# One power for both norms, weight columns by head pair, a rearranged first step and a base laid under the last sum

## The chip, the cores and the metric

The kernel runs on one core of one Trainium2 chip. The metric is device time in microseconds (us) of the whole program; smaller is better. The core's engines each work through their own queue in order: TensorE (PE, with its weight loads shown apart as PEld), VectorE (DVE), ScalarE (ACT), GpSimd (POOL), and SyncE (SP), which here issues all DMAs. They meet only at semaphores.

## What is computed

One transformer layer on x of shape (8, 512, 256) in float32: attention with 16 heads of 64, then a feed-forward block of width 1024 whose output is scaled by a routing weight.

```
xn  = rms_norm(layernorm(x), gamma)          # eps 1e-5 inside the first root, floor 1e-12 on the second norm
q, k, v = split(xn @ w_qkv)                  # 256 x 3072, 16 heads of 64
x   = x + softmax(q*scale @ k.T) @ v @ w_out
y   = layernorm(x)
p   = softmax(y @ router_w); top 2 of 8, normalised; weight = their sum
x   = x + (gelu(y @ w1 + b1) @ w2 + b2) * weight
```

## The kernel before

**Number format.** Every product is made of three TensorE products: each operand is kept as a high part (rounded) and a low part (the rest), and high x high, low x high and high x low are summed in PSUM. So whatever leaves PSUM for a later product costs an ACT copy (the high part, `*_hi`) and a DVE subtraction (the low part, `*_lo`). Softmax probabilities are normalised by POOL before they are transposed.

**Stages.** Eight batches of 512 tokens go through attention one after another; x1 = x + attention is stored in DRAM; then eight batches go through the feed-forward part. Attention works in units n = 0 to 255: one pair of heads times one tile of 128 queries (scores of two heads, 512 keys each). A step holds two units. The order of each engine's queue is written out by hand: in step s, PE runs `transpose_prob(2s-3)`, `scores(2s)`, `scores(2s+1)`, `transpose_prob(2s-2)`, then a "first" auxiliary block, `weighted_values(s-2)` and the "rest" blocks. Auxiliary blocks (`plan_aux`) are the transposes of xn ("xt"), q and k of the next pair, v of the next four heads ("v"), and the product with w_out ("out"). Each has a place that names its PSUM bank (`PS_AUX`). I write t(n) for `transpose_prob(n)` and w(s) for `weighted_values`.

**Prologue.** SP loads x of batch 0 in four tiles, the columns of w_qkv of the first pairs in three groups (`first_stage`, each as two DMAs), identity and gamma, then six 128x768 pieces of w_qkv into `prob`, `wstage` and `halves_out` (which are idle until then). ACT makes high parts (L816, L821), DVE or POOL low parts (L992, L916, L936). PE runs 19 matmuls on zeros (`keep_warm`, L679), and 4 more after the transposes of xn. DVE takes statistics of four x tiles (L967, L971), writes var and var + eps (L973, L974), POOL raises them to +0.5 and -0.5 (L879), DVE makes the scale in four dependent small operations (`attention_scale`, L980 to L984), normalises four tiles (L988). PE transposes them (L574), ACT and DVE split them into `xT`, PE makes k, q, then scores. Units 0 and 1 are followed by q1, k1, both v blocks, then units 2 and 3, then t(0); t(1) waits for the second v block.

**Weights.** `slot_of_chunks` says in which half step a 128x1024 or 128x768 piece is split. Pieces 6 and 7 (w_out) are split in steps 3 and 5: high by ACT, low by POOL. `exp` of the first three units and the first two `copy_halves` wait for the pieces that lie in their buffers.

**Last stage.** For each batch c: eight `up` products, GELU on ACT, high part on POOL (L891), low part on DVE (L992); then four `down` tiles in two PSUM banks, with `transpose_x2` (L628), `route` (L639) and `transpose_logits` (L647) of the next batch between them. `finish` (L1194, L1199) adds b2 to two tiles out of PSUM, then multiplies by the routing weight and adds x1; `store_out` (L456) stores two tiles.

Of the kernel before, what the change touches and what calls it, by code (L numbers as in the profile page):

```python
# [31 lines left out]
P = 128  # L32
# [14 lines left out]
RMS_EPS = 1e-12  # L47
SCALE = DH ** -0.5
# [9 lines left out]
WARM = {FIRST_STEP: 19, -3: 4}  # L58
# [6 lines left out]
PS_AUX = {1: 4, 2: 6, 3: 7, 4: 5}  # L65
# [5 lines left out]
PS_DOWN = (5, 6)  # L71
PS_LAST_OUT = (7, 6, 5, 4)


def plan_aux():
# [3 lines left out]
    for step in range(FIRST_STEP, LAST_STEP + 1):  # L79
        b, rel = divmod(step, SPB_STEPS)  # L80
        blocks = []
        if step == -4:
            blocks += [(1, "xt", 0, 0), (2, "xt", 0, 1)]
# [31 lines left out]
def layer_kernel(nc, x, gamma_cols, w_qkv, w_out, router_w, w1, b1_cols, w2, b2_rows, ident, out):  # L115
# [10 lines left out]
    with ExitStack() as ctx:  # L126
# [20 lines left out]
        halves = sb("halves", [P, 2, TT], F32)  # L147
        ln_stats = sb("ln_stats", [P, TT, 6], F32)
        ln_mv = sb("ln_mv", [P, TT, 2], F32)
        ln_var = sb("ln_var", [P, 2, TT], F32)  # L150
        ln_pow = sb("ln_pow", [P, 2, TT], F32)
        ln_std, ln_rstd = ln_pow[:, 0, :], ln_pow[:, 1, :]
        ln_norm = sb("ln_norm", [P, 3, TT], F32)
# [39 lines left out]
        f_y = sb("f_y", [P, 2, 2, D], F32, ffn)  # L193
# [28 lines left out]
        s_gain = sem("gain_ready")  # L222
        s_q_first_hi = sem("first_query_tile_hi")
        s_q_first = sem("first_query_tile_done")
        s_wload = [sem(f"weights_loaded{i}") for i in range(6)]
# [43 lines left out]
        s_fy = sem("down_read")  # L269
# [11 lines left out]

        N_CONST = 2
        N_CHUNKS = 12

        def weight_chunk(i):

            if i < 6:
                cols, k = i // 2, i % 2
                c = slice(cols * INNER + 2 * P, (cols + 1) * INNER)
                return wqkv_v[:, k, c], [w[:, k, c] for w in wqkv]  # L290
# [9 lines left out]
        stage_of = [0, 1, 2, 3, 4, 5] + [3] * (N_CHUNKS - 6)  # L300
        nth_in_stage = [stage_of[:i].count(stage_of[i]) for i in range(N_CHUNKS)]

        POOL_CHUNKS = (0, 1, 2, 3, 4, 5, 6, 7, 8)
        POOL_HI = (8,)
        slot_of_chunks = {-6: [0, 1], -4: [2], 1: [3], 3: [4], 5: [5], 6: [6], 10: [7]}
# [16 lines left out]
        def weight_stage(i):  # L322
            stage = stage_of[i]
            if stage < NPROB:
                whole = prob[:, stage, :]
            elif stage == NPROB:
                whole = wstage[:, :]
            else:
                whole = halves_out[:, stage - NPROB - 1].rearrange("p a n -> p (a n)")
            return whole[:, 2 * P:] if i < 6 else whole  # L330

        def wait_weight_loaded(eng, i):
            eng.wait_ge(s_wload[stage_of[i]], 16 * (nth_in_stage[i] + 1))
# [7 lines left out]
        def load_weight(sp, i):  # L341
            if nth_in_stage[i]:
                wait_weight_split(sp, max(j for j in range(i) if stage_of[j] == stage_of[i]))
            sp.dma_start(weight_stage(i), weight_chunk(i)[0]).then_inc(s_wload[stage_of[i]], 16)
# [48 lines left out]
        def _(sp):  # L393
            for t in range(TT):
                sp.dma_start(xin[:, t, :], x_v[0][:, t, :]).then_inc(s_x_first[t], 16)
            for k in range(KT):
                sp.dma_start(first_stage[0][:, k], first_source[0][:, k]).then_inc(s_first_load[0], 16)
            sp.dma_start(identity[:, :], ident).then_inc(s_const, 16)
            sp.dma_start(gamma_sb[:, :], gamma_cols).then_inc(s_const, 16)
            for k in range(KT):  # L400
                sp.dma_start(first_stage[1][:, k], first_source[1][:, k]).then_inc(s_first_load[1], 16)
            for k in range(KT):
                sp.dma_start(first_stage[2][:, k], first_source[2][:, k]).then_inc(s_first_load[2], 16)
            for i in range(7):
                load_weight(sp, i)
# [18 lines left out]
            for slot in range(FIRST_SLOT, LAST_SLOT + 1):  # L424
# [25 lines left out]
                for i in weight_slots(slot - 1):  # L450
                    if 6 < i + 1 < N_CHUNKS:
                        load_weight(sp, i + 1)

            def store_out(c, part):
                sp.wait_ge(s_fo, 2 * c + part + 1)
                sp.dma_start(out_v[c][:, 2 * part:2 * part + 2], f_o[:, c % 2, 2 * part:2 * part + 2])\  # L456
                    .then_inc(s_out[c % 2], 16)
# [12 lines left out]
            for i in range(2):  # L470
                sp.wait_ge(s_out[i], 32 * (B // 2))
# [3 lines left out]
        def _(pe):  # L475
# [8 lines left out]
            def scores(n):  # L484

                pair, tile = divmod(n, TT)
                if tile == 0:
                    pe.wait_ge(s_aux, aux_index[("k", pair)] + 1)
                if n == 0:
                    pe.wait_ge(s_q_first, 1)  # L490
# [6 lines left out]
                for q_part, k_part in ((QH, KH), (QL, KH)):  # L497
                    for h in range(2):
                        rows = slice(h * DH, (h + 1) * DH)
                        pe.matmul(ps[:, PS_SCORE[n % 2] + h, :], part[rows, q_part, q0:q0 + P], part[rows, k_part, :],  # L500
                                  start=q_part == QH, stop=False)
                for h in range(2):
# [48 lines left out]

            def aux(step, block_no, place, kind, *args):
# [23 lines left out]
                elif kind in "qk":  # L576
                    pair, = args
                    base = (kind == "k") * INNER + pair % PAIRS * P
                    if pair == 0:
                        pe.wait_ge(s_first_lo, 1)  # L580
                    elif pair == 1:
                        pe.wait_ge(s_first_lo_pool, 1)
                    elif pair == 2:
                        wait_weight_split(pe, 1 if kind == "q" else 3)
                    for k in range(KT):
                        if pair == 0:
                            pe.wait_ge(s_aux, aux_index[("xt", 0, k)] + 1)
                        ins = products(bank, [w[:, k, base:base + P] for w in wqkv],
                                       [v[:, k, :] for v in xT], k == 0, k == KT - 1)
                elif kind == "v":  # L590
# [4 lines left out]
                    elif quad == 1:  # L595
                        wait_weight_split(pe, 5)
# [659 lines left out]
```

## Time and profile before

| | us |
|---|---|
| median of 3 runs | 1207.37 (1205.76 to 1207.79) |
| the profiled execution's own time | 1207.04 |
| its span in the trace | 1205.2 |
| PE busy | 1186.5 (98%) |
| DVE / ACT / POOL busy | 964.6 / 889.3 / 642.7 |

The span is that of the instructions; 1.8 us of the time lie around it. Matmuls are pipelined: a row's duration is longer than the distance to the next one, so starts, not durations, tell what a matmul costs. Attention fills the span from 12 to about 1016 us, the feed-forward part the rest.

### The profile page before, as it was taken

The page shows a single profiled execution, that of the slowest core. Times are in us where ns is not written, and L with a number is a line of the kernel's source. Part 1 is how long each engine was busy: PE and PEld are TensorE (multiplying, and loading weights), DVE is VectorE, ACT ScalarE, POOL GpSimd, SP SyncE. Part 2 cuts the span into 40 slices and gives each one's busy share as a digit, 9 for nine tenths or more (in the row PEclk, how much of TensorE's full clock was granted, in tenths as well). Part 3 has the DMA queues.
Part 4 walks back from the last instruction along what each step waited for, and adds up shares of the span by engine and source line. Part 5 has one row for each costly group of instructions (what it writes and reads, how often), then busy time and mean ns, then how long its engine had stood idle before and what let it go on. Part 6 is the DMA issues. An engine that isn't in the chain of part 4 may idle for free. (4 is left out here: it accounts for less than half of the span.)

```text
span 1205.2 us, 29229 instructions
## 1 busy us (share of the span) xinstructions
PE 1186.5 (98%) x11351; PEld 1038.2 (86%) x11351; DVE 964.6 (80%) x1745; ACT 889.3 (74%) x1921; POOL 642.7 (53%) x802
## 2 busy tenths in 40 slices
PE   8999999999999999999999999999999999999998
PEld 6778888888888888888888888888888888888987
DVE  5789888888888888888888888889888987666644
ACT  5888788878888888888888887888888883344332
POOL 4665556555655565555555655556465664222221
PEclk9999999999999999999999999999999999999999
DMA  4122111311131113111311131113111232111100
GB/s 160 36 56 69 36 36 37 88 37 36 37 88 37 36 37 88 36 36 37 88 36 36 37 88 37 36 36 89 36 36 37 71 89 75 40 59 44 36 19 35
DMA packets 33464, 62.91 MB, mean 52 GB/s; under 512 B 5808, under 2 KB 9904, under 8 KB 33328
## 3 DMA queue, kind: packets, MB, share of 16 engines
q1 hardware_dynamic: 33328, 61.05, 19.8%
q8 instruction: 91, 1.49, 0.5%
q14 instruction: 45, 0.37, 0.1%
HBM read 19.08 MB, written 8.39 MB: 23 GB/s over the span
## 5 line engine op out<-in xcount | busy, mean ns | idle before, releaser
L882 POOL TENSOR_SCALAR prob<-prob,rowinv 128x512 f32<-128x512 f32 x512 | 349.6, 697 | 297.3 <-DVE rowinv L1073 296.6
L790 ACT ACTIVATE prob<-ps,negmax 128x512 f32<-128x512 f32 x512 | 347.2, 686 | 37.8 <-DVE negmax L1068 33.8
L992 DVE TENSOR_TENSOR pT_lo<-ps,pT_hi 128x512 fp32r<-128x512 f32 (+1 forms) x384 | 320.2, 862 | 24.8 <-ACT pT_hi L781 20.2
L1068 DVE TENSOR_REDUCE negmax<-ps 128x2 f32<-128x1024 f32 x256 | 310.9, 1215 | 0.6 <-PE ps L504 0.6
L532 PEld LDWEIGHTS ps<-identity,prob 64*128 64x128 f32 x4096 | 153.8, 138 | 61.5 <-issue 17.3
L778 ACT ACTIVATE pT_hi<-ps 128x1024 fp32r<-128x1024 f32 x128 | 131.5, 1027 | 99.1 <-issue 98.6
L532 PE MATMUL ps<-identity,prob 64*128 64x64 f32 x4096 | 176.6, 226 | 6.2 <-DVE vbuf L992 4.5
L500 PE MATMUL ps<-nat 64*128 64x512 f32 x1024 | 172.4, 413 | 2.4 <-ACT prob L790 0.9
L546 PE MATMUL ps<-pT_hi,vbuf 128*128 128x256 f32 x1024 | 164.6, 283 | 2.6 <-DVE pT_lo L992 2.6
L546 PE MATMUL ps<-pT_lo,vbuf 128*128 128x256 f32 x1024 | 164.1, 283 | 0.0
L781 ACT ACTIVATE pT_hi<-ps 128x512 fp32r<-128x512 f32 x256 | 140.4, 609 | 15.8 <-PE ps L532 15.8
L546 PEld LDWEIGHTS ps<-pT_hi,vbuf 128*128 128x128 f32 x1024 | 144.1, 189 | 9.1 <-DVE pT_lo L992 3.4
L546 PEld LDWEIGHTS ps<-pT_lo,vbuf 128*128 128x128 f32 x1024 | 140.6, 190 | 0.0
L480 PE MATMUL ps<-xT_hi,wbig_hi 128*128 128x512 f32 x320 | 132.9, 415 | 0.3 <-DVE xT_lo L993 0.3
L902 POOL TENSOR_TENSOR att_hi_v<-att_hi_v,att_lo_v 128x512 f32<-128x512 f32 x64 | 83.3, 1301 | 91.7 <-DMA att_lo_v<-halves_out 91.6
L480 PE MATMUL ps<-xT_hi,wbig_lo 128*128 128x512 f32 x320 | 126.9, 397 | 0.0
L480 PE MATMUL ps<-xT_lo,wbig_hi 128*128 128x512 f32 x320 | 126.0, 394 | 0.0
L1073 DVE RECIPROCAL rowinv<-rowsum 128x2 f32<-128x2 f32 x256 | 40.7, 159 | 100.9 <-ACT prob L790 100.8
L790 ACT ACTIVATION_READ_ACCUMULATOR prob<-ps,negmax 128x1 f32 x512 | 103.1, 201 | 0.0
L500 PEld LDWEIGHTS ps<-nat 64*128 64x128 f32 x1024 | 86.9, 187 | 18.4 <-ACT prob L790 6.2
L504 PE MATMUL ps<-nat 64*128 64x512 f32 x512 | 101.8, 393 | 0.0
L891 POOL TENSOR_SCALAR pT_hi<-prob 128x512 fp32r<-128x512 f32 x64 | 40.6, 637 | 103.7 <-ACT prob L809 103.7
(122 smaller groups left out, 2314.6 us busy)
## 6 DMA issues: line engine op xcount, KB each, us to landing
att_hi_v<-halves_out SPq DMA_DIRECT2D x128, 128.0 KB, 2.3
att_lo_v<-halves_out SPq DMA_DIRECT2D x128, 128.0 KB, 2.4
xres<-in_x SPq DMA_DIRECT2D x8, 512.0 KB, 3.5
x_scratch<-xres SPq DMA_DIRECT2D x8, 512.0 KB, 2.7
out_y<-f_o SPq DMA_DIRECT2D x16, 256.0 KB, 2.0
xin<-in_x SPq DMA_DIRECT2D x7, 512.0 KB, 3.8
wstage<-in_w SPq DMA_DIRECT2D x4, 512.0 KB, 3.7
xin<-x_scratch SPq DMA_DIRECT2D x3, 512.0 KB, 3.5
```

Of the source, the lines that this page charges most:

```text
L480: ins = pe.matmul(dst, stationary[i], moving[j], start=first and n == 0, stop=last and n == len(terms) - 1)
L500: pe.matmul(ps[:, PS_SCORE[n % 2] + h, :], part[rows, q_part, q0:q0 + P], part[rows, k_part, :], start=q_part == QH, stop=False)
L504: pe.matmul(ps[:, PS_SCORE[n % 2] + h, :], part[rows, QH, q0:q0 + P], part[rows, KL, :], start=False, stop=True).then_inc(s_score, 1)
L532: ins = pe.transpose(ps[:, bank + r, a * DH:(a + 1) * DH], prob[rows, n % NPROB, a * P:(a + 1) * P], identity[rows, rows])
L546: ins = pe.matmul(ps[:, PS_OUT, h * 2 * P:(h + 1) * 2 * P], vbuf[:, quad % 2, k, pair % 2 * 2 + h, :], pT[part][:, t % 2, h * TT + k, :], ...
L778: act.activation(even_tile(n)[0], two_bank_blocks(PS_PT_EVEN), ACT.Copy).then_inc(s_pthi, 2)
L781: act.activation(odd_tiles(n)[r][0], bank_blocks(PS_PT_ODD + r), ACT.Copy).then_inc(s_pthi, 1)
L790: act.activation(prob[:, n % NPROB, j * SEQ:(j + 1) * SEQ], ps[:, PS_SCORE[n % 2] + j, :], ACT.Exp, bias=negmax[:, n % 4, j:j + 1], accum_ ...
L882: return pool.tensor_scalar(dst, src, scalar, 1.0, ALU.mult, ALU.mult)
L902: pool.tensor_tensor(att_hi_v[:, :], att_hi_v[:, :], att_lo_v[:, :], ALU.add).then_inc(s_head, 1)
L992: return dve.tensor_tensor(dst, full, hi, ALU.subtract)
L1068: dve.tensor_reduce(negmax[:, n % 4, :], ps[:, PS_SCORE[n % 2]:PS_SCORE[n % 2] + 2, :], AX.X, ALU.max, negate=True).then_inc(s_max, 1)
```

## The change

- **One power.** The scale of LayerNorm followed by the RMS norm is written as max(var, floor)^-0.5 and that of the second LayerNorm as (var + eps)^-0.5. DVE writes one number for each tile instead of two, POOL raises 4 instead of 8 for each partition, and `attention_scale` is gone. For batch 0 the statistics and the power are made for tiles 0 and 1, then for tiles 2 and 3.
- **Loads.** Identity and gamma are issued ahead of the first weight columns. The rest of w_qkv comes in six pieces by head pair: q and k of two pairs (128x1024), or v of four heads (128x512), each as two DMAs, into `wstage` or into `xn`, and is split in steps -2, 0, 1, 2, 3 and 5. w_out is split in steps 7 and 9. Both parts of pieces 1 to 8 are made by POOL; `exp` and `copy_halves` wait for no piece.
- **Warm-up.** 12 and 1 matmuls on zeros instead of 19 and 4.
- **First blocks.** `first_product` orders the products of k0 and q0 so that high x high starts when the high part of `xT` is there, and makes the first 128 queries in a bank of their own (5). scores(0) waits for high and low parts one after another.
- **First steps.** q1 and k1, then both v blocks, use banks 4 and 5. PE's order becomes scores(0), scores(1), q1, k1, scores(2), t(0), v part 0, scores(3), v part 1, scores(4), t(1), scores(5), t(2), q2, w(0), k2. ACT, DVE follow.
- **Last stage.** `base` writes b2 * weight + x1 into `f_o` ahead (four operations after `finish(c, 1)` of the batch before); `finish` adds PSUM * weight to it, one operation for each tile. The very last tile has a bank of its own, and tiles 2 and 3 of the last batch are finished and stored apart.

```diff
-WARM = {FIRST_STEP: 19, -3: 4}
+WARM = {FIRST_STEP: 12, -3: 1}
-PS_AUX = {1: 4, 2: 6, 3: 7, 4: 5}
+PS_AUX = {1: 4, 2: 6, 3: 7, 4: 5, 5: 4, 6: 5}
+PS_Q_FIRST = 5
+PS_LAST_DOWN = 3
...
-            blocks += [(3, "v", 0, 0), (4, "v", 0, 1)]
+            blocks += [(5, "v", 0, 0), (6, "v", 0, 1)]
...
-            blocks += [(1, "q", step // 2 + 1), (2, "k", step // 2 + 1)]
+            blocks += [(1, "q", step // 2 + 1), (2 if step else 4, "k", step // 2 + 1)]
...
-        stage_of = [0, 1, 2, 3, 4, 5] + [3] * (N_CHUNKS - 6)
+        stage_of = [0, 1, 0, 1] + [0] * (N_CHUNKS - 4)
-        POOL_HI = (8,)
-        slot_of_chunks = {-6: [0, 1], -4: [2], 1: [3], 3: [4], 5: [5], 6: [6], 10: [7]}
+        POOL_HI = (1, 2, 3, 4, 5, 6, 7, 8)
+        slot_of_chunks = {-4: [0], 1: [1], 3: [2], 5: [3], 7: [4], 11: [5], 15: [6], 19: [7]}
...
+            def first_product(dst, base, queries):
+                for i, j in ((0, 0), (1, 0), (0, 1)):
+                    if (i, j) == (0, 0):
+                        pe.wait_ge(s_first_hi, 1)
+                    if i == 1:
+                        pe.wait_ge(s_first_lo, 1)
+                    for k in range(KT):
+                        if j == 0:
+                            pe.wait_ge(s_auxhi, aux_index[("xt", 0, k)] + 1)
+                        else:
+                            pe.wait_ge(s_aux, aux_index[("xt", 0, k)] + 1)
+                        ins = pe.matmul(dst, wqkv[i][:, k, base:base + P], xT[j][:, k, queries],
+                                        start=i + j == 0 and k == 0, stop=j == 1 and k == KT - 1)
+                return ins
...
-                    pe.wait_ge(s_fy, 2 * (c - 1) + part + 1)
+                    pe.wait_ge(s_fo, 2 * (c - 1) + part + 1)
...
+            SCORE_TILES = {1: (4,), 2: (5,)}
...
-                for n in (2 * step, 2 * step + 1):
+                for n in SCORE_TILES.get(step, (2 * step, 2 * step + 1)):
...
+                    if step == 0 and block_of_aux[2] == "k":
+                        scores(2)
+                        transpose_prob(0)
+                    if step == 0 and block_of_aux[2:] == ("v", 0, 0):
+                        scores(3)
...
                 for block_of_aux in late_blocks(step - 1):
+                    if step == 1 and block_of_aux[2:] == ("v", 0, 0):
+                        transposed_hi(0)
+                        exp(2)
                     aux_hi(*block_of_aux)
+                if step == 1:
+                    exp(3)
...
-                pool.tensor_tensor(ln_pow[:, :, :], ln_var[:, :, :], halves[:, :, :], ALU.pow).then_inc(s_pow, 1)
+                pool.tensor_tensor(ln_scale[:, tiles], ln_var[:, tiles], halves[:, tiles], ALU.pow).then_inc(s_pow, 1)
...
-                if task and task[1] == 4:
-                    powers(task[0])
+                if task == (0, 4):
+                    powers(0, slice(0, 2))
+                    powers(1, slice(2, TT))
+                elif task and task[1] == 4:
+                    powers(task[0] + 1)
...
-                    dve.tensor_copy(ln_var[:, 0, :], ln_mv[:, :, 1])
-                    dve.tensor_scalar(ln_var[:, 1, :], ln_mv[:, :, 1], LN_EPS, None, ALU.add).then_inc(s_var, 1)
-
-            def attention_scale():
+                    tiles = slice(first, last + 1)
+                    dve.tensor_scalar(ln_var[:, tiles], ln_mv[:, tiles, 1], variance, None, op).then_inc(s_var, 1)
...
+            def base(c):
+                if c == 0:
+                    dve.wait_ge(s_b2, 16)
+                if c >= 2:
+                    dve.wait_ge(s_out[c % 2], 32 * (c // 2))
+                for tile in range(TT):
+                    ins = dve.scalar_tensor_tensor(f_o[:, c % 2, tile, :], b2_sb[:, :],
+                                                   r_weight[:, c % 2, tile:tile + 1],
+                                                   f_x1[c % 3][:, tile, :], ALU.mult, ALU.add)
+                ins.then_inc(s_base, 1)
+            def finish(c, part):
+                dve.wait_ge(s_base, c + 1)
+                dve.wait_ge(s_down, 2 * c + part + 1)
+                for tile in (2 * part, 2 * part + 1):
+                    last = c == B - 1 and tile == TT - 1
+                    if last:
+                        dve.wait_ge(s_down, 2 * c + 3)
+                    ins = dve.scalar_tensor_tensor(f_o[:, c % 2, tile, :],
+                                                   ps[:, down_bank(c, tile), tile % 2 * D:(tile % 2 + 1) * D],
+                                                   r_weight[:, c % 2, tile:tile + 1],
+                                                   f_o[:, c % 2, tile, :], ALU.mult, ALU.add)
```

## Rows read from the trace of the kernel before

**Rows 1.** Busy time by stretch: us, PE, PEld, DVE, ACT, POOL busy (xcount), PEclk, DMA, GB/s

```profile
178.00:296.00 118.00, 117.63 (x1205) 103.69 (x1205) 101.15 (x169) 96.39 (x219) 67.85 (x85) 1.00 0.21 51
...
1016.00:1201.00 185.00, 184.88 (x1208) 164.73 (x1208) 108.67 (x309) 68.18 (x90) 45.40 (x62) 1.00 0.12 42
```

**Rows 2.** What PE waited for, 150 to 870 us: us in total, times, longest

```profile
PE ps L532 <- DVE vbuf L992: 1.1, 6, 0.2
```

**Rows 3.** The same view of 0 to 60 us

```profile
PE ps L532 <- DVE vbuf L992: 2.3, 2, 1.9
```

**Rows 4.** Timeline, 4 to 13 us: start, duration, engine, line, operation, out<-in, count [idle before]

```profile
4.79 0.43 DVE L967 BATCH_NORM_STATS2 ln_stats<-xin 128x6 f32<-128x256 f32 x1 [0.32 <-DMA xin<-in_x]
...
5.93 0.63 ACT L816 ACTIVATE wbig_hi<-att_hi_v 128x512 fp32r<-128x512 f32 x1 [3.92 <-DMA att_hi_v<-in_w_qkv]
6.06 1.66 POOL L879 TENSOR_TENSOR ln_pow<-ln_var,halves 128x8 f32<-128x8 f32 x1 [5.21 <-DVE ln_var L974]
...
8.57 1.38 DVE L988 TENSOR_SCALAR xn<-xin,ln_mv,ln_scale 128x256 f32<-128x256 f32 x4
...
10.38 1.27 ACT L744 ACTIVATE xT_hi<-ps,gain 128x512 fp32r<-128x512 f32 x2 [0.88 <-PE ps L574]
...
11.10 1.41 DVE L993 SCALAR_TENSOR_TENSOR xT_lo<-ps,gain,xT_hi 128x512 fp32r<-128x512 f32 x2 [1.07 <-ACT xT_hi L744]
...
12.00 0.47 PE L480 MATMUL ps<-xT_hi,wbig_hi 128*128 128x512 f32 x1 [0.29 <-DVE xT_lo L993]
```

**Rows 5.** Timeline, 13 to 28 us: first k, first scores, first row maxima, t(1)

```profile
13.67 0.60 ACT L757 ACTIVATE nat<-ps 128x512 fp32r<-128x512 f32 x1 [0.55 <-PE ps L480]
...
15.81 0.73 PE L500 MATMUL ps<-nat 64*128 64x512 f32 x4 [0.78 <-DVE nat L993]
...
16.82 2.36 DVE L1068 TENSOR_REDUCE negmax<-ps 128x2 f32<-128x1024 f32 x2
...
27.66 0.71 PE L532 MATMUL ps<-identity,prob 64*128 64x64 f32 x16 [1.95 <-DVE vbuf L992]
```

**Rows 6.** Timeline, 29 to 41 us: scores(5), t(2), t(4)

```profile
29.60 0.73 PE L500 MATMUL ps<-nat 64*128 64x512 f32 x4 [0.48 <-ACT prob L790]
...
30.55 1.04 PE L532 MATMUL ps<-identity,prob 64*128 64x64 f32 x16
...
39.10 0.71 PE L532 MATMUL ps<-identity,prob 64*128 64x64 f32 x16 [0.49 <-DVE nat L992]
```

**Rows 7.** Timeline, 45 to 55 us: a split of w_out on POOL, attention output, probabilities, t(8)

```profile
45.12 2.39 POOL L936 TENSOR_TENSOR wout_lo<-wstage,wout_hi 128x1024 fp32r<-128x1024 f32 x1
...
52.19 2.70 POOL L882 TENSOR_SCALAR prob<-prob,rowinv 128x512 f32<-128x512 f32 x4
...
54.55 0.66 PE L532 MATMUL ps<-identity,prob 64*128 64x64 f32 x16
```

**Rows 8.** Groups by form: count, busy us, mean ns, idle before

```profile
L882 POOL TENSOR_SCALAR wbig_hi<-wstage 128x1024 fp32r<-128x1024 f32 x1 | 1.0, 1040 | 0.0
...
L993 DVE SCALAR_TENSOR_TENSOR nat<-ps,nat 128x384 fp32r<-128x384 f32 x1 | 0.6, 558 | 0.6 <-ACT nat L754 0.6
```

**Rows 9.** Timeline, the warm-up matmuls on zeros

```profile
1.44 6.80 PE L679 MATMUL ps<-pT_hi 128*128 128x512 f32 x19 [1.44 <-DVE pT_hi L963]
```

**Rows 10.** Timeline, 1017 to 1020 us on DVE, the split ahead of the router product

```profile
1017.85 1.23 DVE L992 TENSOR_TENSOR nat<-ps,nat 128x1024 fp32r<-128x1024 f32 x1
```

**Rows 11.** The chain that ended last, 1020 to 1023 us: the router product of batch 1

```profile
1022.02 0.93 PE ps L639 x4
```

**Rows 12.** Timeline, from 1200 us: after the last matmul

```profile
1201.14 0.69 DVE L1194 TENSOR_TENSOR f_y<-ps,b_sb 128x512 f32<-128x512 f32 x1 [4.09 <-PE ps L480]
1201.87 0.88 DVE L1199 SCALAR_TENSOR_TENSOR f_o<-f_y,r_weight,prob 128x256 f32<-128x256 f32 x2
1202.78 0.33 SPq L456 DMA_DIRECT2D out_y<-f_o  x1
```

**Rows 13.** Busy time by stretch: the last store's data

```profile
1203.00:1204.50 1.50, 0.00 (x0) 0.00 (x0) 0.00 (x0) 0.00 (x0) 0.00 (x0) 0.93 0.47 175
```

More of the change, by code:

```diff
@@ L322, in weight_stage @@
         def weight_stage(i):
[L323 to L330, printed above, removed]
+            whole = (wstage[:, :], xn[:, :, :].rearrange("p t d -> p (t d)"))[stage_of[i]]
+            if i >= 6:
+                return whole
+            if i % 2 == 0:
+                return whole.rearrange("p (k c n) -> p k c n", k=KT, c=2)
+            return whole[:, 0:KT * 2 * P].rearrange("p (k n) -> p k n", k=KT)
         def wait_weight_loaded(eng, i):
-            eng.wait_ge(s_wload[stage_of[i]], 16 * (nth_in_stage[i] + 1))
+            eng.wait_ge(s_wload[stage_of[i]], 16 * sum(loads_of[j] for j in range(i + 1) if stage_of[j] == stage_of[i]))
         def wait_weight_split(eng, i):
@@ L450, in _ @@
                 for i in weight_slots(slot - 1):
-                    if 6 < i + 1 < N_CHUNKS:
+                    if 3 < i + 1 < N_CHUNKS:
                         load_weight(sp, i + 1)
             def store_out(c, part):
-                sp.wait_ge(s_fo, 2 * c + part + 1)
-                sp.dma_start(out_v[c][:, 2 * part:2 * part + 2], f_o[:, c % 2, 2 * part:2 * part + 2])\
-                    .then_inc(s_out[c % 2], 16)
+                pieces = 2 if c == B - 1 and part == 1 else 1
+                for i in range(pieces):
+                    sp.wait_ge(s_fo, 2 * c + part + 1 + i)
+                    tiles = slice(2 * part + i, 2 * part + i + 2 // pieces)
+                    sp.dma_start(out_v[c][:, tiles], f_o[:, c % 2, tiles]).then_inc(s_out[c % 2], 16)
             sp.wait_ge(s_pv, STEPS)
@@ L578, in aux @@
                     base = (kind == "k") * INNER + pair % PAIRS * P
-                    if pair == 0:
-                        pe.wait_ge(s_first_lo, 1)
-                    elif pair == 1:
+                    if pair == 1:
                         pe.wait_ge(s_first_lo_pool, 1)
[L583 to L589, printed above, removed]
+                    elif pair in (2, 4, 6):
+                        wait_weight_split(pe, pair - 2)
+                    if pair == 0 and kind == "q":
+                        first_product(ps[:, PS_Q_FIRST, 0:P], base, slice(0, P)).then_inc(s_q_first_full, 1)
+                        ins = first_product(bank[:, P:], base, slice(P, SEQ))
+                    elif pair == 0:
+                        ins = first_product(bank, base, slice(0, SEQ))
+                    else:
+                        for k in range(KT):
+                            ins = products(bank, [w[:, k, base:base + P] for w in wqkv],
+                                           [v[:, k, :] for v in xT], k == 0, k == KT - 1)
                 elif kind == "v":
@@ L786, in exp @@
                     act.wait_ge(s_pt, 2 * (n - NPROB) + 2)
-                else:
-                    wait_weight_split(act, max(i for i in range(N_CHUNKS) if stage_of[i] == n))
                 for j in range(2):
@@ L799, in copy_halves @@
                     act.wait_ge(s_merge, 64 * (pair - 1))
-                if part == 0 and pair < 2:
-                    wait_weight_split(act, 4 + pair)
                 act.activation(halves_out[:, pair % 2, :, part * 2 * P:(part + 1) * 2 * P],
```

210 lines of the change are left out of this document (108 added, 102 removed).

## The prediction

> **What bounds the kernel now.** I read busy time by stretch first. In an attention batch PE is busy 117.6 of 118 us, in the feed-forward stage 184.9 of 185 [rows 1]. Then what PE waited for: from 150 to 870 us six waits of 0.2 us and little else [rows 2]. So in both long stages PE is the bound, no other engine's relief shortens them, and time won ahead of them is kept to the end. What is left are the two ends. At the start PE waits for DVE and ACT [rows 3], and before 12.00 us it has no real work at all [rows 4]; at the end 4.1 us pass between the last matmul (about 1201.1) and the span's end, 1205.2 [rows 12]. The sum is therefore made from the timeline of the two ends, at marks that both kernels have: first xT_hi, first row maximum, t(4), last store.
>
> **Norm, up to xT_hi.** Before: last x tile at 4.79, var at about 5.9, power of 8 numbers 6.06 to 7.72, then four small dependent operations until 8.54, xn from 8.57 to 9.95, xT_hi at 10.38, 0.43 later [rows 4]. After: statistics of tiles 0 and 1 end at about 4.45, those of 2 and 3 at about 5.85 (0.43 a tile, as in the row, plus the same small steps for two tiles). The power of 2 numbers is not in the trace. Bounds: a quarter of 1.66, 0.4 us, if it goes by the element, and all of 1.66 if it is fixed; I take 1.0, between them. With 1.0 the second power ends at 6.9, xn tiles 2 and 3 at 7.75, xT_hi starts at **8.2**, 2.2 us sooner. With 0.4 DVE is the limit (xT_hi 7.8, gain 2.6), with 1.66 twice in a row the second ends at 7.8 (gain 1.35). The identity and gamma DMAs now go ahead of the first weight columns: two issues of some 0.47 us, so these columns, there at 5.93 before, land near 6.9, their high part is made by 7.55 and, behind xn on DVE, the low part by 8.6. The products need them at about 8.9 and 9.5: no cost.
>
> **k0 and q0.** Before, xT_hi 10.38, first product 12.00 (behind the first xT_lo), ACT's k copy 13.67, scores(0) 15.81, row maximum 16.82 [rows 4, 5]. After, the first product starts 0.65 after xT_hi, the last of k0 waits for the second xT_lo (its pair of operations ends 2.13 after xT_hi in the row), so k's copy starts 2.65 after xT_hi instead of 3.29. The queries' first tile has its own bank and is copied while the rest is multiplied; splitting a 512-column product in 128 and 384 adds six short products, 0 to 0.8 us, I take 0.25. The rest of q is then split at about xT_hi + 5.5, and DVE goes to row_max(0) there: xT_hi + 5.6, before + 6.44, gain 0.8. On ACT the high parts of weight groups 1 and 2 (0.63 each) lie between xT_hi and k's copy; they end 0.1 us before it, so a late xT_hi pays nothing, a late load does. First row maximum: 16.82 - 3.0 = **13.8**.
>
> **First steps, to t(4).** From the row maximum to t(4) took 22.3 us before [rows 5, 6]. PE idled in it 1.95 at t(1) (for the second v block, which DVE split only behind two row maxima), 0.48 at scores(5), 0.4 inside t(2) (1.04 instead of 0.66), 0.49 at t(4), with small ones about 3.5 [rows 5, 6]. PE's work is the same after. I laid out the new order with the row durations: scores(2) at 17.65 behind exp(0); t(0) at 18.45, its probabilities normalised 16.9 to 18.25 (POOL must have finished the low part of piece 0 at 16.8: just); v part 0, scores(3), v part 1 until 22.7; scores(4); t(1) waits for DVE's v part at 24.35, 0.9 us idle; scores(5) at 25.05 behind exp(3); t(2), q2 with 0.1 idle, w(0) 28.0, k2 29.9, t(3) 31.45, t(4) 33.55, behind k2's low part. Idle: about 1.2. ACT no longer makes six high parts of 0.85 us, which delayed exactly k2's copy before. So t(4) comes at **33.5 instead of 39.1**, 5.5 us sooner: 2.2 + 0.8 + 2.5.
>
> **POOL's longer splits.** Pieces that ACT and POOL shared are now POOL's alone: a full piece costs 1.04 more than its 2.39 [rows 7, 8]. They stand in steps 3, 7 and 9, where normalise(n) and the attention output queue behind them, and t(8), t(16) and t(20) wait for that. Before, with 2.39 in step 3, the probabilities of unit 8 were ready at 53.5 and t(8)'s second half needed them at 54.9, 1.4 us of slack [rows 7]. 1.04 more leaves 0.3, and POOL's own predecessor is won only 5.0 us, not 5.5. I charge 0.2 to each of three places, 0.6 in all (0 to 2.0). Pieces 1, 3 and 5 are half as wide, and xn and `wstage` are reloaded only behind their splits: SP stands at these waits, but what is queued behind it (the load of x of batch 1, the first regrouping) is due microseconds later. Cost nothing.
>
> **Norms of batches 1 to 7, and the second one.** Five small DVE operations go, about 1 us a batch, and the power halves. The waits of [rows 2] do not lie in those steps. Gain 0 (up to 1.1, if DVE's lead helps them).
>
> **Last stage.** `base` is four operations of 0.44 on DVE, 1.8 us, against 1.4 of the dropped `f_y`; DVE is busy 109 of 185 us there. Two places could feel it. In batch 0 it stands ahead of the split that the router product needs: this ended at 1019.1 and becomes 1020.9, the product starts at 1022.0 [rows 10, 11]. Behind `finish(c, 1)` it moves the first hidden_lo: DVE is then free 2.7 us after the last down product instead of 1.6, while the first hidden tile needs 1.4 for its product and 0.7 each for GELU and the high part. Nothing. PE waits for `s_fo` instead of `s_fy`, 0.2 later, for a bank it wants 12 us later.
>
> **The very end.** Before: 0.69 + 0.88 with gaps, 1.64 from 1201.14 to the issue [rows 12]. After: one operation on 128x256 out of PSUM, 0.44 as in the row, below the 0.56 of a 384-column one [rows 8]: 0.47, gain 1.17 (1.05 to 1.2). The last store carries half the bytes: its data occupied 0.47 of 1.5 us, 0.7 [rows 13], half of which is 0.35; bounds 0 and 0.4. Together **1.45**.
>
> **Sum.** 2.2 + 0.8 + 2.5 - 0.6 + 1.45 = 6.35. The profiled execution, 1207.04 with 1.8 us around its span, becomes 1200.7. It lies 0.33 below the median, 1207.37, and this becomes **1201.0**.
>
> **The warm-up.** The 19 matmuls of 512 columns take 6.80 us [rows 9]. At the distance of the later k products, 0.23 to 0.25 (six in the 1.67 us from 12.00 to the copy [rows 4, 5]), they would take 4.6, so some ran at half rate: 1.2 GHz puts them 0.43 apart, 2.4 GHz about half. Eleven at 0.43 and eight at 0.23 make 6.6 us, which puts the change near 6.2. The granted clock reads 1.00 all along; only the spacing tells. Twelve matmuls end at about 6.6, only 0.4 behind that change. Until the first product at 8.9 PE has eight transposes and one more matmul, a gap of 2.3 us; before, it had the same gap between 8.24 and 10.53, and the products that followed ran at full speed. I take the clock as up.
>
> The Trainium skill (TensorE: Matmul & The Clock Gate, Part 4) says that a transpose "doesn't count as PE-busy the same way". It speaks against the smaller warm-up. The row agrees neither way: one execution, in which the gap did no harm. By that rule the result would be the first rival's.
>
> **Rivals.** (1) *The clock is low for k0 and q0.* For: the rise is 0.4 us from the end of the warm-up, in one execution. Against: the equal gap before. Price: k0's four late products 0.2 more each, q0's six of 384 columns 0.15 more each, about 1.9 in all: 1202.9. If it lasts through step 0, 2 more. (2) *DVE and ACT are later in steps 0 to 3 than laid out, or POOL is.* t(0) has no slack behind POOL, t(1) and t(3) hang on the order of DVE. One wait of each of the sizes seen before (0.5) at four places: 1203.0. (3) *The split pieces put POOL on the path, slower.* Place: steps 1 to 10. Two steps give POOL 15 us, of which probabilities take 5.5 and an attention output 3.3; a full split takes 3.4, so it fits. It decides from the point where one split no longer clears before the next unit's probabilities are due; then all of them would be on the path, 3 x 3.4 + 3 x 2.0 = 16 us: 1217. Speaks against it: 1.4 us of slack seen with 70% of that load. (4) *The head start isn't kept*: the step that loads xn and `wstage` only behind their splits makes q2 or the first regrouping late, and all but the end's 1.45 is lost: 1205.9.
>
> **How the numbers follow.** Forecast 0.64 (its own range 1199.3 to 1202.3, from the power's bounds +-0.6, POOL 0 to 2.0, the store), rival 1 0.14, rival 2 0.15, rival 4 0.04, rival 3 0.03. The range that holds 8 in 10 takes in both middle rivals: 1199.3 to 1203.8. 0.2% is 2.4 us, about what a measurement of this kernel can tell from no change: faster means below 1204.95. Faster 0.93, same 0.04, slower 0.03.
>
> **What would show it.** xT_hi at 7.8 to 9.0; two powers and their length; the first row maximum near 13.8; a wait of about 1 us at t(1) instead of 1.95; t(4) near 33.5; no wait of PE for POOL's probabilities above 0.3 at t(8), t(16), t(20); about 117.6 busy in a later batch; 0.5 us from the last matmul to the last store. Wrong would be: matmuls 0.43 apart after 9 us, a row maximum behind 15, or a batch in the middle that is longer than before.

## The result and the profile after

The changed kernel takes 1198.25 us in the median (1198.14 to 1198.65), the kernel before 1207.15 (1205.76 to 1207.79) when timed beside it: a ratio of 0.9928, 95% interval 0.9911 to 0.9946. (One execution of the kernel before, timed beside the later experiments, took 2255.91 us and is left out below.) The forecast was 1201.0 with a range from 1199.3: the direction was right, and the time lies 1.1 us below the range. The profiled executions give the same gain, 1207.04 to 1198.14, 8.90 us where the sum had 6.35, and they show where it was won.

Busy time and span of the changed kernel, from its page:

```profile
span 1196.3 us, 29198 instructions
PE 1183.7 (99%) x11347; PEld 1040.4 (87%) x11347; DVE 961.9 (80%) x1714; ACT 884.3 (74%) x1914; POOL 640.1 (54%) x809
```

The shares are within a point of those before. PE had 1186.5 us there. Up to the first product it now has 2.97 us less, with ten warm-up matmuls fewer; from the first GELU on 1.3 less; in between 1.4 more. The totals don't tell where 8.9 us went, marks on the timeline do.

Its timeline from 4 to 14 us (columns as in [rows 4]), lines of POOL, ACT, PE and DVE, engine by engine:

```profile
4.51 0.72 POOL L924 TENSOR_TENSOR ln_scale<-ln_var,halves 128x2 f32<-128x2 f32 x1 [3.69 <-DVE ln_var L1023]
5.57 0.79 POOL L924 TENSOR_TENSOR ln_scale<-ln_var,halves 128x2 f32<-128x2 f32 x1 [0.34 <-DVE ln_var L1023]
...
7.56 1.27 ACT L792 ACTIVATE xT_hi<-ps,gain 128x512 fp32r<-128x512 f32 x2 [0.58 <-PE ps L610]
...
10.34 0.60 ACT L805 ACTIVATE nat<-ps 128x512 fp32r<-128x512 f32 x1 [0.45 <-PE ps L584]
...
8.39 0.99 PE L584 MATMUL ps<-xT_hi,wbig_hi 128*128 128x512 f32 x2 [0.20 <-ACT xT_hi L792]
...
13.08 1.22 DVE L1111 TENSOR_REDUCE negmax<-ps 128x2 f32<-128x1024 f32 x1
```

The power took 1.66 for 8 numbers a partition [rows 4]; for 2 it takes 0.72 to 0.79. xT_hi starts at 7.56 instead of 10.38, the first product at 8.39 instead of 12.00, the first row maximum at 13.08 instead of 16.82 [rows 5].

PE's transposes t(1) to t(4), from the timeline of 24 to 35 us:

```profile
24.18 0.71 PE L552 MATMUL ps<-identity,prob 64*128 64x64 f32 x16 [0.65 <-DVE vbuf L1035]
25.53 0.66 PE L552 MATMUL ps<-identity,prob 64*128 64x64 f32 x16
31.21 0.71 PE L552 MATMUL ps<-identity,prob 64*128 64x64 f32 x16
33.21 0.66 PE L552 MATMUL ps<-identity,prob 64*128 64x64 f32 x16
```

The wait at t(1) is 0.65 instead of 1.95, and t(4) comes at 33.21 instead of 39.10 [rows 5, 6]: 5.89 us won.

The end of the changed kernel:

```profile
1193.53 0.48 DVE L1254 SCALAR_TENSOR_TENSOR f_o<-ps,r_weight,f_o 128x256 f32<-128x256 f32 x1 [2.32 <-PE ps L495]
1194.04 0.33 SPq L472 DMA_DIRECT2D out_y<-f_o  x1
```

From the start of DVE's last work to the span's end 2.77 us, before 4.06 [rows 12]: 1.29 won.

Of the 8.90 us the two ends explain 7.18. The rest is found by the lag: how much sooner each mark comes in the changed kernel than in the one before.

```
mark            lag, us (before minus after)     forecast, us
xT_hi           2.82                             2.2
row maximum     3.74   (+0.92)                   +0.8
t(4)            5.89   (+2.15)                   +2.5
t(21)           6.13   (+0.24)                   -0.6
first GELU      6.00   (-0.13)                   0
last GELU       7.73   (+1.73)                   0
DVE's last work 7.61   (-0.12)                   0
end of the span 8.90   (+1.29)                   +1.45
```

The last stage, in which PE is 100% busy in both kernels [rows 1], became 1.6 us shorter. That is the question the experiments begin with. The chain that ended last shows it in one batch of that stage (start, duration, line, matmuls). After:

```profile
1083.87 5.75 PE ps L495 x48
...
1093.77 13.97 PE ps L495 x72
```

Before:

```profile
1091.04 5.64 PE ps L480 x48
...
1100.81 14.25 PE ps L480 x72
```

The x72 are 48 products of 512 columns (up, hidden from xT or nat) and 24 of 256 (down); the x48 are down products alone. The x72 group is 0.28 faster after, the x48 group 0.11 slower, though the change touched no instruction in either. In distances from start to start, in the mean over six batches: 512 columns 233 ns before and 227 after, 256 columns 120 and 122.

### The profile page after: what moved, and what is told of

Read it like the earlier page. It is cut to its first block and busy times, and to the rows that moved or that the text cites. A ratio compares the mean times of both kernels' runs of the same rounds, so it can differ in the third digit from the quotient of the medians.

```text
span 1196.3 us, 29198 instructions
## 1 busy us (share of the span) xinstructions
PE 1183.7 (99%) x11347; PEld 1040.4 (87%) x11347; DVE 961.9 (80%) x1714; ACT 884.3 (74%) x1914; POOL 640.1 (54%) x809
## 3 DMA queue, kind: packets, MB, share of 16 engines
HBM read 19.08 MB, written 8.39 MB: 23 GB/s over the span
## 5 line engine op out<-in xcount | busy, mean ns | idle before, releaser
L495 PE MATMUL ps<-xT_hi,wbig_lo 128*128 128x512 f32 x316 | 124.4, 394 | 0.0
L495 PE MATMUL ps<-xT_lo,wbig_hi 128*128 128x512 f32 x316 | 123.1, 389 | 0.0
```

Source lines behind the costliest of these rows:

```text
L495: ins = pe.matmul(dst, stationary[i], moving[j], start=first and n == 0, stop=last and n == len(terms) - 1)
```

## Experiments

### Where the buffers lie

The small tiles of the norm become fewer and smaller in the change, and so every buffer allocated behind them, xT, nat and pT among them, lies 96 bytes lower in SBUF. Theory A: PE's rate depends on the address of its operands (A2, the form it took after the first runs: on the address modulo 256). Rival B: the old last stage itself slows PE, by the traffic of `f_y`. The expectations also speak of C, on the clock, which comes below. They give the changed kernel's batch as 24.65 us; measured between the first GELUs of batches it is 24.746. Two paddings of the changed kernel first; e1:

```diff
         ln_scale = sb("ln_scale", [P, TT], F32)
+        pad = sb("pad", [P, 8], F32)
```

> The changed kernel with one unused tile of 32 bytes a partition behind ln_scale, so that every buffer allocated later (xT, nat, prob, pT, vbuf) starts 32 bytes higher; nothing else. In the last stage the changed kernel takes 24.65 us a batch where the kernel before takes 24.88, with the same products: up's 512-column products start 227 ns apart instead of 231 to 238, down's 256-column ones 120 instead of 118. The smaller norm buffers moved all later buffers down by 96 bytes, from a start that is 32 beyond a multiple of 64 to a multiple of 64. Theory A (the place of the operands in SBUF sets the distance): a batch takes 24.88 again, down's products are 118 apart, the time is 1200.0 (1.7 more than 1198.25). Rival B (the dropped f_y pass and its traffic, or the new wait, made PE faster): nothing moves, 1198.3, 24.65 a batch.

Measured: 1198.77 us (1197.90 to 1199.25), the last stage's batches 24.873 us apart instead of 24.746. One unused tile of 32 bytes gives up nearly the whole difference to the kernel before (24.887). The whole time rose by 0.5 us, though, not by the 1.7 expected.

e2, the same tile further on, so that only pT and what follows moves:

```diff
         prob = sb("prob", [P, NPROB, 1024], F32)
+        pad = sb("pad", [P, 8], F32)
```

> The changed kernel with the unused 32 bytes between prob and pT: xT and nat stay at multiples of 64, pT, vbuf, w_out and attT start 32 beyond one. Theory A, if the moving operand decides for up (xT, nat) and the stationary one for down (pT): up stays at 227 ns, down goes to 118, a batch takes about 24.65 - 96 x 0.002 = 24.46, the last stage is 1.5 us shorter, 1196.8; the products with v and w_out in attention go the way of the kernel before (119 instead of 120), up to 2 us more. If theory A holds only for the moving operand, the last stage stays at 24.65. Rival B: 1198.3.

Measured: 1196.92 us (1196.59 to 1197.33), batches 24.613 apart. The up products stay fast and the down products become fast too, if less than expected (24.46): this beats both kernels, by 1.3 us the changed one.

e3, the 32 bytes of e1 in the kernel before:

> The kernel before with the same unused 32 bytes behind ln_scale, nothing of the change. Theory A: a batch of the last stage takes 24.65 instead of 24.88, up 227 ns apart, down 120; the attention stage, whose two kinds of products cancelled, stays within 0.5; 1205.4, 1.7 less than 1207.15. Rival B: 1207.15, 24.88.

Measured: 1206.73 (1205.90 to 1208.94), batches 24.88: no change in the last stage where theory A, in its first form, wanted 24.65. A multiple of 64 is not what makes up fast.

e4, the kernel before with the new last stage (`base`, one operation at the end, the last tile in its own bank, half a store), addresses as before:

> The kernel before with the last stage of the change alone: base, finish in one operation a tile, the last tile in a bank of its own, the last two tiles stored apart. Forecast's term: 1.45 less; the trace of after has 2.77 us from the end of the last product's wait to the end of the span where before has 4.06, so 1.3 less. Theory A: buffers up to attention lie as before, a batch stays at 24.88, 1205.85 in all. Rival B: the last stage is 1.7 shorter as well, 1204.1.

Measured: 1205.87 (1205.24 to 1207.73), a ratio of 0.9988 (0.9978 to 0.9997), batches 24.852. The last stage's new order brings its end, 1.3 us from DVE's last work to the end of the span, and 0.035 us a batch, not the 0.141.

e5, the kernel before with a pad of 160 bytes, and e6, the changed kernel with one of 128 bytes; they cross the two theories:

```diff
         ln_scale = sb("ln_scale", [P, TT], F32)
+        pad = sb("pad", [P, 40], F32)      # e5;  e6: [P, 32]
```

> The kernel before with 160 unused bytes a partition behind ln_scale. After e1 to e3: up's 512-column products start 227 ns apart in the two kernels whose xT begins at 83072, 232 to 234 in those where it begins at 83104, 83168 or 83200. 160 bytes put it at 83328, which like 83072 is 128 beyond a multiple of 256, while 83200 is a multiple of 256. Theory A2 (the place modulo 256 decides): up 227, down 120, a batch of the last stage 24.7 instead of 24.88. Theory B2 (both kernels with 227 also have the new last stage; its missing f_y pass gives it): up stays at 232.

> The changed kernel with 128 unused bytes there: xT at 83200, as in e3. Theory A2: up 232 and down 119 or 120 apart, a batch about 24.95, 1199.8 to 1200.2. Theory B2: up stays at 227, 1198.3.

The chain in e5, the old code at the new code's place:

```profile
1091.25 5.75 PE ps L481 x48
...
1101.15 13.97 PE ps L481 x72
```

and in e6, the new code at another place:

```profile
1083.76 5.70 PE ps L496 x48
...
1093.57 14.20 PE ps L496 x72
```

e5 has the changed kernel's 5.75 and 13.97 to the last digit, with the old last stage and all of `f_y`'s traffic; e6 has 14.20 with the new one. Rival B falls, A2 stands for the last stage. All layouts together (the start of xT_hi and of pT_hi in bytes beyond a multiple of 256, nat lies like xT; median distances over six batches, where before has one in six at 238; one batch of the last stage):

```
kernel     xT   up, ns     pT   down, ns   batch, us
before    224   231       224   118        24.887
e1        160   234       160   117        24.873
e3          0   232         0   119        24.88
e6          0   232         0   119        24.880
e5        128   227       128   120        24.746
after     128   227       128   120        24.746
e2        128   227       160   117        24.613
```

The layout of the last row but one is also that of e7 to e11 below, and their batches are 24.746 to 24.759 apart. e2 separates pT from xT and nat. What no run separates is xT and nat from the other buffers that move with them (xin, xres, xn, prob): that up's distance goes by the address of its own moving operand, and not by that of a buffer which another engine uses meanwhile, is argued and not shown.

In whole times e5 (1206.95, ratio 1.000, 0.9991 to 1.0009) and e6 (1197.96, 1196.52 to 1198.99) show nothing of it: with the last stage alone e5 would be 1.2 us below the kernel before, and e6 was expected at 1199.8 to 1200.2. Whether the place acts on attention the other way can't be told. From the row maximum of unit 60 to that of unit 252 it took 732.42 us in e5, 731.32 in e6, 732.20 before and 732.12 after; but in the changed kernel and e7 to e11, which share layout and code there, it took 731.17 to 732.25. What is shown is the last stage's own rate. From the first GELU to DVE's last work e5 is 1.2 us shorter than before (206.2 against 207.4). The changed kernel is another 0.4 shorter, nearly all in the stage's first batch, whose first GELUs run beside the end of attention (36.71 us to the second batch's first GELU in e5, 36.26 after). That part stays open: PE waits there for DVE's last addition to `xres`, 0.32 before and 0.17 in e5, and not after; but e3 has no such wait either and takes 36.69, e4 with the new last stage 36.83, and e11 with the changed kernel's code 36.68.

### The first steps and the clock

e7 puts the order of steps 0 to 2 back (v blocks, scores and exponentials as before) and keeps all else.

> The changed kernel with the order of steps 0 to 2 as before (banks of v, k1; units 2 and 3 behind both v blocks; t(0) behind them; ACT and DVE likewise). The forecast's term for the order is 2.5. Theory: PE waits about 2 us at t(1) again, t(4) at 35.6 instead of 33.2, 1200.7 in an execution whose clock stays. Theory C (the granted clock fell to 0.5 from 28.4 to 31.8 us in e3 and from 29.0 to 35.8 in e4, behind two microseconds at t(1) in which PE was 0.2 to 0.6 busy): some executions lose it here too, about 25 us, and are 1 to 2.5 us longer, so that the runs scatter by 2 us where those of the changed kernel scatter by 0.5. Rival: the order isn't worth more than the waits listed, and no execution loses the clock: 1200.3 to 1200.8 with a scatter of 0.5.

Measured: 1200.52 (1199.62 to 1202.21), 2.3 us lost where the expectation had 2.45; t(4) at 35.21. Theory C was that PE's wait of about 2 us at t(1) lets the clock fall in some executions. PE of e7 around it:

```profile
24.21 1.07 PE L552 MATMUL ps<-identity,prob 64*128 64x64 f32 x16 [1.95 <-DVE vbuf L1027]
25.04 1.20 PE L518 MATMUL ps<-nat 64*128 64x512 f32 x4
```

Its busy time and granted clock by 2 us (columns: us, PE, PEclk, DMA, GB/s):

```profile
24.00:26.00 2.00, 1.79 (x20) 0.57 0.46 182
26.00:28.00 2.00, 2.00 (x20) 0.57 0.00 0
28.00:30.00 2.00, 2.00 (x22) 1.00 0.00 0
```

The same of e3, which has the order of before:

```profile
26.00:28.00 2.00, 0.59 (x18) 1.00 0.94 243
28.00:30.00 2.00, 1.79 (x14) 0.61 0.50 189
30.00:32.00 2.00, 2.00 (x23) 0.54 0.00 0
```

and of the changed kernel:

```profile
24.00:26.00 2.00, 1.82 (x38) 1.00 0.48 186
26.00:28.00 2.00, 1.85 (x15) 1.00 0.00 0
```

After a wait of 1.95 us at t(1), the granted clock is 0.5, that is 1.2 instead of 2.4 GHz, for 3.4 us in e3, e5 and e7 and for 6.8 in e4. It falls with t(1) in e7 and 1.0 to 2.2 us after its start in the others. In e7 the sixteen transposes take 1.07 instead of 0.71, four score products 1.20 instead of 0.71. In the profiled execution of before the clock stayed up behind the same wait. In no profile with the new first steps does a row show such a fall.

The granted clock that is on record for every execution says the same. e4 and e7 have the change's last stage but the old first steps: 12 of their 15 executions read below 1.0 in the mean (0.997 to 0.999). Of 38 executions with the new first steps none does but e9's profiled one, which reads 0.949. Of 42 executions of the kernel before those that read 1.0 took 1206.5 us in the mean, those at 0.998 or 0.999 1207.4, those at 0.997 1208.6; a part of that reading can come from its longer end, where the clock is at 0.5 too. So part of the old order's price is a risk. The scatter alone doesn't show it: e7's is 2.6 us and the changed kernel's 0.5, but e6's is 2.5 at a clock of 1.0 throughout, and e7's fastest execution, the profiled one, is one in which the clock fell.

e11 leaves the warm-up out (`WARM = {}` instead of 12 and 1 matmuls on zeros), to price the forecast's first rival.

> The changed kernel with all warm-up matmuls on zeros left out (12 and 1). It prices the forecast's first rival. If the clock is low for k0 and q0: granted clock 1.0 only behind the first products, k0's and q0's 512-column products 0.43 apart instead of 0.23, first row maximum 1.5 to 2.5 later than 13.08 (14.6 to 15.6), possibly more into step 0; time 1199.8 to 1202. Rival: the clock is up on its own, or the row maximum hangs on DVE: the maximum stays at 13.1 and the time within 0.3 of 1198.25.

Measured: 1200.69 (1199.91 to 1201.26), so 2.4 us lost. Its PE:

```profile
9.00 1.56 PE L584 MATMUL ps<-xT_hi,wbig_hi 128*128 128x512 f32 x2
10.35 1.05 PE L584 MATMUL ps<-xT_hi,wbig_lo 128*128 128x512 f32 x2
```

Pairs of 512 columns take 1.05 where the changed kernel's took 0.62 to 0.63, the first row maximum comes at 15.78, 2.7 later, and all of it is kept: t(4) and the first GELU are 2.7 to 2.8 later too. The rival's price, 1.9, was slightly low; 0.6 of the 2.7 is a later xT_hi (8.16). The granted clock reads 1.00 all along here as well, so only the spacing tells.

With the twelve matmuls and the one that the change keeps, the products run at full speed in every profile. When the clock rises differs from execution to execution. The warm-up of the changed kernel:

```profile
1.44 4.60 PE L717 MATMUL ps<-pT_hi 128*128 128x512 f32 x12 [1.44 <-DVE pT_hi L1012]
```

and the same twelve in e7:

```profile
1.44 5.49 PE L717 MATMUL ps<-pT_hi 128*128 128x512 f32 x12 [1.44 <-DVE pT_hi L1004]
```

In nine profiles, before among them, the distance changes from 0.43 to 0.23 us inside the warm-up, between 4.5 and 6.3 us. In e1, e7, e8 and e9 all twelve are 0.43 apart, so the rise came behind them, and yet k0's products, which begin between 8.5 and 9.4 us, come as in the changed kernel, from the third on 0.23 to 0.24 us apart. The forecast took one execution's 6.2 for the kernel's. How few matmuls would do, no run here shows.

### Power, first products

e8 makes one power of 4 numbers for batch 0 instead of two of 2.

> The changed kernel with one power for all four tiles of batch 0, behind the statistics of all four. The power took 0.72 us for 2 numbers a partition and 1.65 for 8, so 1.03 for 4 if it is a line. Theory (all of the chain up to xT_hi is on the path): statistics end at 5.55, power at 6.6, xn from 6.65 to 8.0, xT_hi at 8.45 instead of 7.56, and 0.9 is lost at the end, 1199.15. Rival (the first weight columns or the warm-up are as late): less than 0.4 lost.

Measured: the power of 4 takes 1.04 us, xT_hi starts at 8.57 (expected 8.45), t(4) is 1.08 later. The time, 1198.82 (1198.22 to 1199.61), is only 0.57 above. The profiled execution comes 1.14 us later than the changed kernel's at t(21) and 0.10 at t(215), in steps that both share; e7, e10 and e11 gain 0.3 to 0.7 in the same stretch, so it is the scatter of single executions in attention. What is shown is the delay at the first marks; that 0.9 of it reaches the end is not. With 1.66 for 8, 1.04 for 4 and 0.72 to 0.79 for 2 the power costs 0.15 us a number and about 0.43 to begin.

e10 gives k0 and q0 their old products' order (wait for both parts of xT, block by block).

```diff
-                for i, j in ((0, 0), (1, 0), (0, 1)):
-                    ... wait for s_first_hi, s_first_lo or xT's own part as each is needed
-                    for k in range(KT):
+                pe.wait_ge(s_first_lo, 1)
+                for k in range(KT):
+                    pe.wait_ge(s_aux, aux_index[("xt", 0, k)] + 1)
+                    for i, j in ((0, 0), (1, 0), (0, 1)):
```

> The changed kernel with one part undone: the products of k0 wait for both parts of the first block of xT and for the low part of the weights, in the old order of products (hi*hi, lo*hi, hi*lo of one block, then of the next). Forecast's step (k copy 2.65 after xT_hi instead of 3.29): the first product starts 0.7 to 0.9 later (9.1 to 9.3), k's copy at 10.9 to 11.0 instead of 10.34, first row maximum 13.6 to 13.7 instead of 13.08, t(4) 33.7 to 33.9, time 1198.25 + 0.6 = 1198.85. Rival: the q tile of its own bank and DVE set the row maximum, not k: the maximum stays at 13.1 to 13.2 and the time within 0.3 of 1198.25.

Measured: 1198.79 (1198.59 to 1199.30), first product at 9.29, k's copy at 10.96, row maximum at 13.68, t(4) 33.82. All within 0.1 of the expectation: +0.6 at the marks from k's copy on and +0.54 in the time.

### POOL's longer splits

The lag falls by 0.12 at t(8), by 0.32 at t(16) and by 0.34 at t(20): the three places where the forecast charged 0.2 each. PE and POOL of the changed kernel there:

```profile
48.19 1.04 PE L552 MATMUL ps<-identity,prob 64*128 64x64 f32 x16
...
47.34 2.71 POOL L927 TENSOR_SCALAR prob<-prob,rowinv 128x512 f32<-128x512 f32 x4
```

t(8) takes 1.04 instead of 0.66 [rows 7]: after eight transposes PE stands 0.33 us until POOL's second tile (47.34 + 2 x 0.67) is there. The view of waits does not name it, since it lies inside a group. In t(8) the gap stands where the kernel before waited 0.46 behind the transposes, so little is lost; in t(16) and t(20) more is. e9 gives the high parts of these three pieces to ACT, with a semaphore of its own:

```diff
-        POOL_HI = (1, 2, 3, 4, 5, 6, 7, 8)
+        POOL_HI = (1, 2, 3, 5, 8)
+        ACT_HI = (4, 6, 7)
```

> The changed kernel with one part undone: the high parts of the three full pieces of steps 3, 7 and 9 are made by ACT again (its own semaphore), POOL makes only their low parts. In the changed kernel t(8), t(16) and t(20) take 0.81 us from the first to the last matmul of their sixteen, with one gap of 0.33, where 0.43 to 0.49 is usual and where the kernel before has 0.43 to 0.49; the third probability tile of each is ready just as the gap ends. POOL theory (the forecast's 0.2 at each of three places): all three go back to 0.43 to 0.49, PE comes out of t(21) some 0.75 us sooner (98.7 instead of 99.44), the time is 1198.25 - 0.7 = 1197.5. Rival, the work only moves: ACT's copies of about 1 us hold up a softmax or a copy in the same steps, PE waits there instead, t(21) stays within 0.2 of 99.4 and the time is 1198.0 to 1199. Rival two, the gaps have another cause: they stay.

Measured: 1199.97 (1199.50 to 1200.37), 1.7 us slower. The rival was nearer (1198.0 to 1199), and it too was too low. PE and ACT of e9:

```profile
49.36 0.66 PE L560 MATMUL ps<-identity,prob 64*128 64x64 f32 x16
...
41.83 0.71 PE L560 MATMUL ps<-identity,prob 64*128 64x64 f32 x16 [1.11 <-DVE vbuf L1044]
...
39.39 1.05 ACT L872 ACTIVATE wbig_hi<-wstage 128x1024 fp32r<-128x1024 f32 x1
40.34 0.65 ACT L819 ACTIVATE vbuf<-ps 128x256 fp32r<-128x256 f32 x2
```

Both theories are right in their half. The gap is gone in all three units (0.66 again), so POOL made it. But ACT's 1.05 us stands ahead of its copy of the v block, and PE waits 1.11 for it at t(6), and t(6), t(14) and t(18) come 0.94 later each, 2.8 in all. Without POOL's gaps 0.31, 0.30 and 0.61 of that are won back behind t(8), t(16) and t(20). With the 0.35 that e9 brought along from the start t(21) is 1.94 later. POOL's lateness costs up to 1.2, ACT's 2.8: the changed kernel's choice is the cheaper one.

e12 puts e9's edit on e2's layout.

> The changed kernel with both improvements found: 32 bytes between the probabilities and pT (as in the run that took 1196.92), and the high parts of the three full pieces on ACT. If both causes are separate and each is real they add up: 1196.92 - 0.7 = 1196.2, batches of the last stage 24.61 us apart, t(8), t(16), t(20) at 0.43 to 0.49. If the high parts only move work: 1196.7 to 1197.3.

Measured: 1198.18 (1197.90 to 1198.61), 1.26 above e2 where the expectations had 0.7 less or up to 0.4 more, with the last stage's batches at 24.633 and the same three waits: the last stage's rate goes by the place whatever the first steps do, and e2 stays the fastest.

## Why the prediction was wrong where it was

- **The step that failed** is the first one: "in both long stages PE is the bound, no other engine's relief shortens them", and with it the term 0 for the last stage, the largest miss. That PE is the bound is right. That nothing but its count of matmuls sets its time was assumed: the edit moved PE's operands by 96 bytes, and the same matmuls ran at another distance. Measured 1.6 us for that stage, 1.2 of it from the place (e5), the rest in its first batch and of open cause. With it the forecast would have been 1199.4. This is an account of profiled executions by their marks. The whole times don't bear it out: e6, whose last stage has the old rate, took 1197.96 and so lies below the range as well. In its profile the last stage is 0.9 us longer than in the changed kernel's, and attention (from t(21) to the first GELU) 0.8 shorter.
- **Norm**, forecast 2.2, measured 2.82. The mechanism held. xT_hi came at 7.56, not 8.2: 0.33 of it because the second power could start at 5.57 instead of 5.9 (the statistics of tiles 2 and 3 ended at 5.49, not 5.85), 0.21 because it took 0.79 and not 1.0, 0.1 behind it. The earlier statistics are also why the end of the range (2.6) was passed. The lower bound "a quarter of 1.66" was too low, since the power has a fixed part (e8).
- **k0 and q0**, forecast 0.8, measured 0.92; the order of products is 0.6 of it (e10). The clock was up for the products, so rival 1 did not come. Its price of 1.9 is near the 2.1 which e11 shows beside the later xT_hi, but the two terms that the forecast names for it make 1.7; the six products of 128 columns are not among them.
- **First steps**, forecast 2.5, measured 2.15; e7 takes 2.3 us back by undoing them. The wait at t(1), forecast 0.9, was 0.65. t(4), laid out for 33.5, came at 33.21.
- **POOL**, charged 0.6. The three places and the cause were right (e9), the sizes 0.12, 0.32 and 0.34 of lag instead of 0.2 each, 0.78 in all. Against it stood what the sum had left out: the kernel before lost 0.28, 0.31 and 0.30 at t(5), t(6) and t(10), which the changed one does not; why the one before lost them is open. The forecast stopped its layout at t(4) and took the lead as constant from there. Rival 3's avalanche did not come.
- **The very end**, forecast 1.45, measured 1.29; the operation took 0.48 (0.47 forecast), and 1.13 of the gain lie before the store's issue, so the smaller store was worth 0.16, not 0.35.
- The terms that failed add up: +0.62 +0.12 -0.35 +0.84 (t(4) to t(21)) -0.13 +1.61 -0.16 = 2.55, the difference of 8.90 and 6.35.

Whether the place acts in attention, and why single executions of one layout differ there by 1.1 us, is not settled: the last stage gives clean numbers, attention's total does not. What in the chip makes up faster with xT and nat 128 bytes beyond a multiple of 256, and down with pT 32 beyond a multiple of 64, no run here tells.

## What to carry to other kernels

Where PE is the bound and the buffers move, the time of its products may move with them: compare the distance from start to start of the same products in both traces, and try a pad of 32 bytes before an edit is credited with the difference. Lay out the new order until the lag is constant, not until the last step that was edited, and look inside groups of transposes for gaps that no view of waits names. A wait of 2 us early in a kernel can cost more than its length, if the clock falls behind it: read the granted clock of every execution, not of the profiled one alone.

## What the runs showed of the hardware

- In the last stage a 512-column fp32r product starts 227, 231 to 232 or 234 ns (medians) after the last one, depending on where xT and nat lie; a 256-column one 117 to 118, 119 or 120 depending on where pT lies (seven kernels, above). The Trainium skill (TensorE: Matmul & The Clock Gate, Part 2, Back-to-back issue gap) gives the isolated gap by the column count alone, some 216 ns for 512. The medians here lie 11 to 18 above it, and nothing in it varies with the place.
- The granted clock fell to 0.5 behind PE's 1.95 us at t(1), in four of the five profiles with that wait (e3, e4, e5, e7) and not in before's. At the start it rose between 4.5 us and the products of k0, at another time in each execution. One profile (e9) reads 0.95 from end to end; its batches of the last stage are 24.759 us apart, 24.746 in the changed kernel, so that reading cost next to nothing.
- The changed kernel's twelve warm-up matmuls were followed by eight transposes and one more matmul, and the 512-column pairs of k0 took 0.62. The Trainium skill (TensorE: Matmul & The Clock Gate, Part 4) says of a transpose that it "doesn't count as PE-busy the same way". With the twelve and the one ahead of the products the runs show no harm from it; with transposes alone (e11) the products ran at half speed, which fits the sentence but doesn't prove it.
- POOL's power: 1.66, 1.04 and 0.72 to 0.79 us for 8, 4 and 2 numbers a partition.
